# A gated attention block in float32: a new hand-written order of work on every engine

## The reference

```
h  = layernorm(x)
x1 = x + tanh(g_xattn) * (dequant(fp8(h)) @ dequant(fp8(ctx)).T)     # blocks of 128, 4 partial products
f  = layernorm(x1) @ (Wa * column scales)                            # 512 x 1536
q, k, v per head (16 heads of 32; the last 8 columns swapped between q and k where w_rec > 0.1)
out = x1 + tanh(g_ffn) * (softmax(causal(q k^T / sqrt(32))) @ v) @ Wp
```

## Time and profile before

| | us |
|---|---|
| median of 3 runs | 531.11 |
| the profiled execution | 531.24 |
| its span, first to last instruction | 529.5 |
| TensorE busy | 458.1 (87%) |
| VectorE busy | 336.6 (64%) |
| ScalarE busy | 272.3 (51%) |
| GpSimd busy | 144.5 (27%) |
| mean granted TensorE clock | 0.959 |

### The profile page before, as it was taken

The page is one execution under the profiler, slowest core; times in us unless marked ns, Lnnn a source line. Parts: engine busy times, 40 slices in busy tenths (PEclk is TensorE's granted clock), DMA queues, the critical chain, the costliest instruction groups (busy, mean ns, idle before and its releaser), DMA issues.

```text
span 529.5 us, 7878 instructions
## 1 busy us (share of the span) xinstructions
PE 458.1 (87%) x2536; PEld 325.8 (62%) x2536; DVE 336.6 (64%) x1110; ACT 272.3 (51%) x530; POOL 144.5 (27%) x264
## 2 busy tenths in 40 slices
...
GB/s 232 165 34 48 158 85 105 81 49 96 145 2 2 71 105 159 95 35 101 138 19 2 51 104 136 125 26 99 98 6 2 45 102 93 82 95 106 22 20 80
DMA packets 28025, 42.62 MB, mean 80 GB/s; under 512 B 8272, under 2 KB 8528, under 8 KB 27984
## 3 DMA queue, kind: packets, MB, share of 16 engines
...
q10 hardware_dynamic: 1536, 0.14, 0.2%
...
## 4 chain that ended last, share of the span: by engine, by line
PE 58%; ACT 18%; DVE 13%; SPq 3%; issue 3%; DMA 2%; POOL 2%; ACTq 1%; DVEq 0%; POOLq 0%
PE pv_bank L716 11%; PE mm_bank L564 7%; PE mm_bank L565 6%; PE mm_bank L566 6%; PE exp_bank L702 5%; DVE x_all L1201 5%; PE max_bank L685 5%; ACT work L984 4%; DVE max_bank L1235 3%; SPq L374 3%; PE mm_bank L743 2%; PE mm_bank L744 2%; PE mm_bank L745 2%; PE turn_bank L580 2%; ACT tile_buf L931 2%
## 5 line engine op out<-in xcount | busy, mean ns | idle before, releaser
L1235 DVE CUSTOM_DVE_ANT_0 max_bank<-max_bank,causal 128x512 f32<-128x512 f32 (+3 forms) x256 | 119.2, 517 | 65.4 <-PE max_bank L685 65.0
L482 POOL TENSOR_SCALAR_AFFINE_SELECT work<-work 128x384 f32<-128x384 f32 x64 | 33.4, 521 | 299.4 <-ACT work L984 299.4
L984 ACT ACTIVATE work<-exp_bank 128x512 f32<-128x512 f32 (+1 forms) x192 | 90.9, 526 | 25.5 <-PE exp_bank L702 24.5
L716 PE MATMUL pv_bank<-work,v_aug 128*33 128x256 f32 (+3 forms) x512 | 83.6, 473 | 0.0
L702 PE MATMUL exp_bank<-q_stack,k_stack 97*128 97x512 f32 (+3 forms) x256 | 68.9, 353 | 4.1 <-ACT work L984 1.6
L685 PE MATMUL max_bank<-k_stack,q_stack 96*128 96x512 f32 (+3 forms) x256 | 61.7, 342 | 10.4 <-DVE row_max L1235 6.5
L716 PEld LDWEIGHTS pv_bank<-work,v_aug 128*33 128x33 f32 x512 | 29.0, 118 | 54.2 <-issue 48.5
L1218 DVE SCALAR_TENSOR_TENSOR qk_lo<-mm_bank,col_root,qk_hi 128x512 fp32r<-128x512 f32 x32 | 24.0, 750 | 59.2 <-ACT qk_hi L957 59.1
L1201 DVE SCALAR_TENSOR_TENSOR x_all<-mm_bank,coef,x_all 128x128 f32<-128x128 f32 x224 | 61.0, 342 | 0.8 <-PE mm_bank L612 0.8
L685 PEld LDWEIGHTS max_bank<-k_stack,q_stack 96*128 96x128 f32 x256 | 45.9, 196 | 17.8 <-issue 7.0
L702 PEld LDWEIGHTS exp_bank<-q_stack,k_stack 97*128 97x128 f32 x256 | 43.3, 188 | 19.7 <-ACT work L984 9.0
...
## 6 DMA issues: line engine op xcount, KB each, us to landing
q_stack<-qk_hi SPq DMA_DIRECT2D x128, 64.0 KB, 2.0
k_stack<-qk_hi SPq DMA_DIRECT2D x128, 64.0 KB, 2.0
...
```

Source lines behind the costliest of these rows:

```text
L482: pool.affine_select(out=three, in_=three, compare_op=ALU.is_ge, fill=0.0, base=0, pattern=[[0, 3], [1, P]], channel_multiplier=-1)
L716: last = pe.matmul(pv_bank[64 * j:64 * j + D + 1, P * m:T], v_aug[:, m, 2 * u + j, :], prob[j][:, PROB_COL[m]:PROB_COL[m] + T - P * m], st ...
L984: act.activation(prob[j][:, UNIT_COL[k]:UNIT_COL[k] + UNIT_LEN[k]], exp_bank[(3 * j + k) % 2][:, 0:UNIT_LEN[k]], ACT.Exp, scale=SCALE).the ...
L1235: last = dve.tensor_tensor_reduce(max_bank[unit % 2][:, col:col + width], max_bank[unit % 2][:, col:col + width], causal[:, T - width:T], ...
```

## The change

The order of work changes on TensorE, ScalarE, VectorE and GpSimd; SyncE's list is as it was. No instruction is added or removed in what is computed. In the gap lists the names move to other gaps, and products are cut into parts of 3, 6 or 9 matmuls. In the prologue the calls that were written out become lists too (`PE_FIRST`, `ACT_FIRST`, `DVE_FIRST`, `POOL_FIRST`) in another order, with a loop that maps each name to the call that stood there before. VectorE also waits once for the four low parts of the prologue before it starts the batches.

```diff
 PE_GAPS = [
-    ["W0 v3", "W1", "Q2", "K2"],
-    ["", "W2", "W3", ""],
-    ["Q3", "", "", "X0"],
-    ["K3 S0 S1", "S2 X1", "S3 S4 S5", "X2"],
-    ["S6 S7", "S8 S9 S10", "", "S11 X3"],
-    ["S12 H0 S13", "", "S14 S15", ""],
-    ["H1 A0", "", "H2", ""],
-    ["A1 H3", "q0 k0", "q1", ""],
+    ["W0 v3.012", "Q2.0 v3.3", "Q2.1 W1", ""],
+    ["Q2.23 K2.01 W2", "W3", "K2.23", "Q3.0"],
+    ["Q3.123", "K3.0", "X0", "K3.123 S0"],
+    ["S1", "S2 S3 X1", "S4 S5 X2 S6 S7", ""],
+    ["S8", "", "X3 S9 S10", ""],
+    ["S11 S12", "", "S13 S14 H0", ""],
+    ["S15 H1 A0", "", "H2", ""],
+    ["A1 H3", "q0 k0", "q1.01", ""],
 ]
 ACT_GAPS = [
-    ["", "W0", "", "", "v3 Q2", "W1"],
-    ["", "L0 K2", "", "W2 L1", "", "L2"],
-    ["L3", "C0", "", "W3", "", "X0 C1"],
-    ["Q3", "K3", "", "", "X1 C2", ""],
-    ["X2", "", "C3", "", "", ""],
-    ["N0 X3", "", "", "H0", "N1", "H1"],
-    ["", "", "", "N2", "H2", ""],
-    ["N3", "H3 c0 q0", "", "k0", "q1", ""],
+    ["", "", "", "v3 W0", "", ""],
+    ["", "W1 Q2 L0 W2 L1", "", "L2", "", "L3 K2"],
+    ["", "Q3 W3 C0", "", "", "C1", "X0 K3"],
+    ["", "C2", "", "X1 C3 X2", "", ""],
+    ["", "", "", "", "", "X3 N0"],
+    ["N1", "", "", "", "H0", "H1"],
+    ["", "", "", "N2", "H2", "N3"],
+    ["", "H3", "", "q0 k0", "", "q1 c0 c1 c2"],
 ]
 DVE_GAPS = [
-    ["", "", "x0 x1 x2 x3", "", ""],
-    ["Q2", "", "", "", "m0 m1 e0 m2 K2 m3"],
-    ["", "", "", "", ""],
-    ["e1", "Q3 K3 S0 S1", "S2", "S3", "S4 S5 S6"],
-    ["", "S7 b0 S8", "b1", "S9 S10", "S11"],
-    ["t0", "t1 S12 t2 S13 b2", "", "H0 t3", "S14 S15"],
-    ["b3 A0", "H1", "", "", ""],
-    ["", "H2 A1 H3 q0 k0 q1", "", "", ""],
+    ["", "", "", "x0", "x1"],
+    ["x2 x3 Q2", "", "", "", "m0 m1 m2 e0 m3 K2"],
+    ["", "", "Q3 e1", "", "K3"],
+    ["", "S0 S1", "S2 S3 S4 S5", "", "S6 b0"],
+    ["S7", "S8 b1", "", "", ""],
+    ["S9 S10 S11 t0 t1 S12", "t2 b2", "", "", ""],
+    ["t3 S13 H0 S14 S15 b3 A0", "H1", "", "", "H2"],
+    ["", "A1", "H3 q0", "k0", "q1 k1"],
 ]
...
 PE_LAST = [
-    ["v3", "Q2", "K2", "Q3"],
-    ["", "", "", "K3"],
-    ["", "", "Y0", "Y1"],
-    ["", "Y2", "", "Y3"],
-    ["", "", "z0", "Y4"],
-    ["", "Y5", "z1", "Y6"],
-    ["", "", "", "Y7"],
-    ["z2", "Z0", "Z1", "Z2 Z3"],
+    ["v3.012 Q2.0 v3.3", "Q2.1", "Q2.23 K2", "Q3.012"],
+    ["Q3.3", "", "K3.0", "K3.1"],
+    ["K3.23", "", "", "Y0"],
+    ["", "", "z0", "Y1"],
+    ["", "", "z1", "Y2"],
+    ["Y3", "Y4", "Y5", "Y6 Y7"],
+    ["", "", "", "Z0"],
+    ["", "Z1", "z2", "Z2 Z3"],
 ]
...
-PE_END = "k1 P0 M0 V0 T0 V1 M1 y0 y1 y2 M2 V2 y3 O0 O1 O2 O3"
-ACT_END = "k1 T0 c1 V0 c2 y0 V1 y1 y2 V2 c3 y3"
-DVE_END = "k1 M0 T0 M1 y0 M2 y1 O0 y2 O1 y3 O2 O3"
+PE_FIRST = ("f0 f1 f2 f3 f4 S0 S1 S2 S3 f5 S4 S5 S6 f6 S7 S8 S9 S10 f7 S11 f8 S12 S13 f9 "
+    "S14 S15 v0 v1 f10 f11 q0 B0 k0 V2 B1 q1 M0 k1 M1 M2")
+ACT_FIRST = ("L0 L1 L2 L3 C0 C1 C2 d0 f0 C3 C4 f1 f2 C5 f3 b0 f4 b1 a0 a1 f5 C6 a2 a3 "
+    "C7 f6 f7 N0 b2 f8 b3 N1 f9 v0 N2 N3 f10 f11 q0 v1 k0 V2 q1 p0 c0 c1 c2 k1 "
+    "c3")
+DVE_FIRST = ("x0 x1 x2 x3 t0 t1 t2 t3 A0 w0 A1 T0 T1 T2 F0 F1 T3 F2 F3 c0 S0 S1 S2 S3 "
+    "S4 S5 S6 b0 S7 b1 S8 S9 u0 S10 S11 h0 S12 S13 S14 S15 b2 b3 h1 u1 u2 h2 h3 u3 "
+    "B0 q0 k0 B1 q1 M0 M1 M2 k1")
+POOL_FIRST = "i0 s0 s1 s2 s3 o0 s4 s5 s6 l0 l1 s7 l2 l3 r0 j0 j1 j2 r1 j3 g0 g1 g2 g3 p0"
+PE_END = "q1.23 k1.01 P0 V0.0 k1.23 V0.1 M0 V0.2 T0 V0.3 V1.01 M1 y0 V1.23 y1 V2.0 M2 V2.123 y2 y3 O0 O1 O2 O3"
+ACT_END = "T0 k1 y0 V0 y1 V1 V2 y2 y3 c3"
+DVE_END = "M0 T0 M1 y0 M2 y1 O0 y2 O1 y3 O2 O3"
```

More of the change, by code:

```diff
@@ L1058, in _ @@
-            qk_split_hi(1, 1, 0, first=True)
-            for k in range(NT):
-                cast(1, k)
+            for kind, i in pieces(ACT_FIRST, True, True):
+                if kind == "L":
+                    layernorm_x(0, i, first=True)
+                elif kind == "C":
+                    cast(0, i, first=True)
+                elif kind == "f":
+                    first_hi(i)
+                elif kind == "d":
+                    act.wait_ge(s_gates, 32)
+                    act.activation(gates[:], gates[:], ACT.Tanh).then_inc(s_tanh, 1)
+                elif kind == "a":
+                    weight_hi(i)
+                elif kind == "b":
+                    weight_tail_hi(i)
+                elif kind == "N":
+                    layernorm_x1(0, i)
+                elif kind == "v":
+                    first_values(i)
+                elif kind == "V":
+                    side("V", i, 0)
+                elif kind == "p":
+                    act.wait_ge(s_wload[NK], 16)
+                    act.activation(wp_hi[:], raw_wp, ACT.Copy).then_inc(s_wphi, 1)
+                elif kind == "c":
+                    cast(1, i)
+                else:
+                    if kind == "q" and i == 0:
+                        act.wait_ge(s_root, 1)
+                    qk_split_hi("qk".index(kind), i, 0, first=True)
@@ L1209, in x1_stat @@
                 dve.bn_aggr(mv2[:, i, :], bn2[:, i, :]).then_inc(s_x1, 1)
-            def first_sum(i):
-                for k in range(NK):
-                    add_sum(0, i, k, first=True)
-                x1_stat(0, i)
             def qk_split_lo(w, g, n):
```

264 lines of the change are left out of this document (112 added, 152 removed).

## The result

The changed kernel takes 513.63 us (median of four runs, 512.06 to 513.97) against 530.55 (527.91 to 533.79) for the kernel before on the same chip: a ratio of 0.967 with a 95% interval of 0.961 to 0.973, so 3.3% faster. The forecast was 525.2 with a range of 516.5 to 532.8: the sign was right, and the gain is nearly three times as large and outside the range. Every ratio in this document is to the kernel before on the same chip, and leaves out executions more than 1.5% above the fastest of their kernel, so it can differ a little from that of the two medians.

What follows compares the result with a forecast made beforehand. Each middle batch was taken as bound by TensorE, then VectorE, then TensorE. Batches -1.4, -2.3 and -2.7, prologue +0.3 and last batch +0.2 summed to -5.9 us: 525.2 from a median of 531.11, range 516.5 to 532.8.

Steps and rivals of the forecast that it cites:

- Prologue, "+0.3": Prologue: early delays on VectorE and GpSimd mostly absorbed by room later in the chain; +0.3 us, bounds -2 and +3.
- R4: Prologue: the swap mask's nine small loads land late and hold everything behind it; up to 4 us, 529; chance 0.05.
- the earlier k1 doesn't matter: Prologue after q0: TensorE would again wait 2.67 us for SyncE's stack transfers, so having k1 sooner gains nothing.
- The mask, row or rule: Prologue swap mask on VectorE: 1.08 us by the profile row, about 0.3 by the shared-interface rule, then prologue 0.5 better.
- Steps 0 to 2, "+2.2": Each middle batch: 2.97 us more TensorE work, 0.75 filled into idle time; +2.2 us, bounds +1.9 and +3.5.
- cutting a product costs nothing by itself: Products on TensorE: same 12 matmuls on the same bank, weights loaded for each anyhow; cuts only hide latency.
- Steps 3 to 6, "-3.6, -4.5, -4.9": Middle batches 0, 1, 2: less VectorE work and idle time cut to 1.5 us, giving 42.9, 42.9 and 40.1 us.
- R1: Middle batches: larger gain, VectorE idle falling to 0.6 us and slow clock met less; 7.6 us more, 517.6; chance 0.2.
- Step 7 and the end, "0": End of the middle batches: same products, values and turns, little idle time to gain; 0, bounds -1.5 and +1.
- Last batch, "+0.2": Last batch: same TensorE work in other steps, 1.4 us less cover in step 7; +0.2 us, bounds -1 and +1.5.
- R2: Middle batches: new waits replace K3's, VectorE's idle stays 3.2, 4.2 and 4.6 us; 532.8, half of it about 530; chance 0.18.
- R3: Steps 3 to 6: less TensorE work brings the slow clock, TensorE decides; +6.3 us each batch, 544; chance 0.07.

## Why the prediction was wrong, point by point

**Prologue, "+0.3": the step that failed. By the run with the prologue alone it is wrong by 7.5 us, with an interval of 4 to 11.** Its parts up to q0 were near enough: the three tails took 1.74 us each (16.72 to 21.93) for 1.9, and the small loads landed late, which was R4: 2.23 us of wait in this execution, 1.0 to 2.3 in all eight with the early mask. What failed is the sentence "the earlier k1 doesn't matter". I followed the chain to q0 and then to the transfer before step 1's scores, where TensorE waited 2.67 us before and 3.59 after, and took the start of step 0 as the end of the matter. The stretch from k1 through ScalarE's casts to the first row maxima had no row in my list. In all five profiles of the old prologue ScalarE takes the maxima out 3.3 to 4.4 us after TensorE turned them, with the new one 0.3 to 0.8 us after; step 0 of batch 0 took 13.85 us with the one and 9.83 with the other under the same middle lists. And the earlier trace rows held one execution of a prologue that takes 85.4 to 88.9 us. The one I had was the shortest of five.

**The mask, row or rule.** It took 0.23 us with GpSimd waiting, not 1.08. The Trainium skill (GPSIMD Engine Reference, section 1, Specifications) says that the two engines share their SBUF interfaces; the trace agrees, as the weight tail's predicated copy beside GpSimd's scaling took 1.05, as before. It gave nothing, since the loads came later than either.

**Steps 0 to 2, "+2.2": mis-sized, and its reason wrong.** Against the earlier trace rows it was +0.8, +1.6 and +1.7. I had 2.97 us of work, 0.75 filled, and the sentence "cutting a product costs nothing by itself" read only one way: it also gives by itself, since a cut product can be spread. K3 early without cuts costs 3.4 us; whole products under the new lists cost 1.7 us more than cut ones (1.3 in batch 0). One hole of 0.72 us is most of what the view counts as idle there; the rest is counted as busy, so the 0.7 us of idle time in the earlier trace rows was no bound on what could be filled. A small part of that shows in the means: in batch 1 the 512-column scores for the maxima have 411 ns with whole products and 393 with cut ones, six of them.

**Steps 3 to 6, "-3.6, -4.5, -4.9": right in mechanism, mis-sized.** It was -5.0, -5.4 and -6.3. VectorE's work came out as summed (40.90, 41.03, 38.13 for 41.4, 41.4, 38.6); its idle time was 0.6, 1.0 and 0.6 where I took 1.5. That is R1's own condition, and the wait of 1.46 that I kept went with the slow value product. That VectorE bounds the stretch is shown by the run with the context's work moved out, where it shortens by as much as VectorE's work.

**Step 7 and the end, "0": wrong against this profile.** -2.0, -2.0 and -1.4. I had seen the slow value product of step 6 and not the one of 4.04 us behind it. But the experiments split this term: the old lists reach 42.5 as well, so 0.3 of it is the order and 1.7 the clock in that one stretch. In batches 0 and 1 the profiles with the old end lists lose it in 5 of 10 cases, those with the new ones in 5 of 18, and the changed kernel's own in neither; so a part of that 1.7 may be luck of this execution.

**Last batch, "+0.2".** 0.2 us slower with the lists alone, interval -1.7 to +2.2 by its ratio: right.

**Rivals.** R2 (paid back) and R3 (slower by the clock) are out: VectorE has no new wait of a us in steps 3 to 6, and TensorE at 0.92 there in batch 1 cost at most 0.6 us (42.0, where the middle lists alone took 41.4 at 1.00). R1's conditions came true: idle time of 0.6 to 1.0, and no slow value product in this execution. The middle lists alone gave 11.5 us, 5.1 more than forecast and between the forecast's 1.4 + 2.3 + 2.7 = 6.4 and R1's 6.4 + 7.6 = 14.0; 519.8 lies in the range, and it was the prologue that took the time out of it.

**Still open:** which of the prologue's new orders brings the maxima in time; how much of the gain is the clock that executions differ by; and what makes step 7 fall to 0.96. It did so after steps 3 to 6 at 0.92 (whole products in steps 0 to 2) and at 0.96 (short statistics), but the changed kernel's batch 1 came out of 0.92 with 1.00.
